# A three-layer decoder block in one Trainium2 core: the value products of two units stand together behind every second score step

## The chip, the cores and the metric

The kernel runs on one core of a Trainium2 chip (trn2). Its time is that of one execution on the device in microseconds (us). The engines are named PE (TensorE; its weight loads are PEld), DVE (VectorE), ACT (ScalarE), POOL (GpSimd) and SP (SyncE, which here only issues DMAs). Each has its own instruction queue, worked off in order, and waits on semaphores that the others raise. The kernel was timed in three runs.

## The reference

Four sequences of 1024 tokens, width 256, 16 heads of 16, all in float32:

```
x = x + self_attention(layernorm(x))      # causal, each chunk of 128 queries sees its own
                                          # 128 keys and those of the chunk before it
x = x + cross_attention(layernorm(x), ctx_1024)   # 77 keys per sequence, masked per query
x = x + ffn(layernorm(x))                 # 8 bit fake-quantised gate, up and down, 704 wide
```

Both attentions are `softmax(q k^T / 4) v` per head, followed by an output projection.

## The kernel before

**Stages.** The attention layers of all four sequences are worked off as sixteen jobs, in the order S0a S0b S1a S1b S2a X0a S2b X0b S3a X1a S3b X1b X2a X2b X3a X3b: S is self attention, X cross attention, the digit is the sequence, and a or b says which eight heads. A job has two phases, g = 0 and g = 1, of four heads each. The feed-forward layer follows when all jobs are done and is not touched here.

**A unit.** In a phase the score matrices are computed transposed (keys on partitions), in units: a self phase has 8 units of 128 keys by 256 queries by 4 heads, a cross phase 4 units of 77 keys by 256 queries by 4 heads. For a unit the step `score` makes four bfloat16 matmuls on PE (L699; cross L706 with a mask matmul L709), ACT takes the exponential out of the two banks into a buffer `pt` (L974, cross L978), and in self attention POOL zeroes what is above the diagonal (L1451). The step `val` then multiplies the exponentials with the values: four float32 matmuls with 17 output columns each (16 of the head and one of ones, which gives the sum), one for each quarter of 32 columns of the PE array (`tile_position=(0, 32 * i)`), at L737 for self and L748 for cross. A float32 matmul is two instructions in the trace, so a unit shows as x8. Unit 3 of a self phase is cut in two halves of 128 queries and shows as x16, unit 7 has only 128 queries. They accumulate in two banks of their own, which ACT copies out after unit 3 (or 1) and after the last one (`evac`, L987).

**What else stands between.** The row maxima of the next phase are found ahead of its scores: score matmuls in the other orientation (`max`, L667 and L670; cross L677 and L679), reduced on DVE (L1179, L1183), turned and sent by ACT's DMA into the rows 96 to 98 of the queries, where the scores subtract them. The projections for the jobs to come (L630, L640), layer normalisation, the output projection (L759), and the weights of the feed-forward layer fill the rest.

**What sets the order.** `attention_order()` writes one list of steps, and every engine works off its part of it in that order. A phase is given a length (24.5 for S, 9.6 for X), and each kind of step a span in it as fractions, in `PLACE`; all steps are sorted by the time that this gives. `score` step j stands at j/8 or j/4 of the phase. `val` of unit j - 2 stands right behind `score` j (`BEHIND["val"]` is 2), and the last two units of a phase, its tail, stand at the span `tail` of the next phase. There are three buffers `pt` (`NPT`), and an exponential waits until the `val` of the score step three before it has been made. In `follow()` further steps are hung behind a step by a number of steps (`norm`, `proj`, `rows`, `acc`, `fin`).

**The keys of cross attention.** The step `xkeys` projects the values of the cross keys (PE L649, DVE adds the bias at L1169, POOL sets the ones at L1446); DVE and POOL wait there for the last `val` of the job before the running one. The step `bulk` copies queries and keys into one of four slots by six DMAs on SP (L523 from `parts`; the cross keys L517 from `kparts`). `PLACE["keys x"]` places `xkeys` and the key copy for g = 0 of the next cross job, where the running job is a cross one; there are four such places (jobs X2a, X2b, X3a and X3b are the next).

Of the kernel before, what the change touches and what calls it, by code (L numbers as in the profile page):

```python
# [6 lines left out]
F32 = mybir.dt.float32  # L7
# [9 lines left out]
KX = 77  # L17
FI = 704
FT = 6
NPT = 3  # L20
NEG = -1.0e30
EPS = 1e-5
SCALE = 0.25
# [3 lines left out]
        for j in "S0a S0b S1a S1b S2a X0a S2b X0b S3a X1a S3b X1b X2a X2b X3a X3b".split()]  # L27
# [5 lines left out]
PLACE = {"max s0s": (-0.001, 0.635), "max s1s": (-0.31, 0.27), "max s1x": (-0.071, 0.513),  # L33
# [6 lines left out]
         "score x": (0.078, 1.077), "shift": (0.305, 1.038), "setup": (0.177, 0.8), "v first": (-0.574, 0.433),  # L40
         "qk first": (0.482, 0.895)}

BEHIND = {"scaled": 3, "turned": 3, "scaled 4": 0, "split": 1, "vmove": 0, "bulk": 13, "turnm": 3, "evac": 4,
          "spread": 2, "gather": 2, "invert": 5, "store": 2, "widen": 8, "scale": 8, "wturn": 2, "val": 2}

# [40 lines left out]
class Order:  # L86
# [5 lines left out]
    def put(self, s):  # L92
        if s[0] == "force":
            while any(g == s[1] for _, g, _ in self.due):
                it = next(it for it in self.due if it[1] == s[1])
                self.due.remove(it)
                self.put_one(it[2])
            return
        self.put_one(s)
        ready = []  # L100
        for it in list(self.due):
            it[0] -= 1
            if it[0] < 0:
                ready.append(it)
        for it in ready:
            if it in self.due:
                self.due.remove(it)
                self.put_one(it[2])
# [12 lines left out]
def over(span, steps):  # L121

    return [(span[0] + (span[1] - span[0]) * i / len(steps), step) for i, step in enumerate(steps)]
# [43 lines left out]
def attention_order():  # L167
# [19 lines left out]
    def put(steps):  # L187
        timed.extend(((start + t * length, len(timed) + i, step) for i, (t, step) in enumerate(steps)))

    for p in range(2 * len(JOBS)):  # L190
# [1 line left out]
        job, units = JOBS[n], UNITS[JOBS[n][0]]  # L192
        kind, length = job[0], LENGTH[job[0]]
        nxt = JOBS[n + 1] if n + 1 < len(JOBS) else None
        put([(-0.001, ("force", "rows"))] + over(PLACE["tail " + kind], tail))
        scores = over(PLACE["score " + kind], [("score", job, g, j) for j in range(units)])
        for j in range(units):
            put([scores[j]])
            if j >= BEHIND["val"]:
                put([(scores[j][0] + 0.002, ("val", job, g, j - BEHIND["val"], False))])  # L200
        tail = [("val", job, g, j, j == units - 1) for j in range(units - BEHIND["val"], units)]
        if p + 1 < 2 * len(JOBS):
            put(over(PLACE[f"max {kind}{g}{nxt[0] if g else kind}"], max_steps(p + 1)))
        last = JOBS[n - 1] if n else ("s", 0, 0)
# [70 lines left out]
def build(nc, x_in, ctx_in, mask_in, w_qkv, w_out, Wq, bq, Wk, bk, Wv, bv, Wo, bo, clip_x, clip_d, w_gate, w_up,  # L275
          w_down, out):
    with ExitStack() as ctx:
        def sb(name, shape, dt):
            return ctx.enter_context(nc.sbuf_tensor(name, shape, dt))
# [8 lines left out]
        ring = big[:, 0:16384].bitcast(BF16).rearrange("p (r z h t) -> p r z h t", r=4, z=2, h=4)  # L288
        qs = [ring[:, r, 0] for r in range(4)]
        ks = [ring[:, r, 1] for r in range(4)]  # L290
        pt = [big[:, 16384 + 1024 * i:17408 + 1024 * i] for i in range(NPT)]
        rem = big[:, 19456:20480].rearrange("p (i n) -> p i n", i=2)
        va = [big[:, 20480 + 1088 * f:21568 + 1088 * f].rearrange("p (c h d) -> p c h d", c=NC, h=8)
              for f in range(2)]
# [1249 lines left out]
```

How the kernel before makes its waits and increments, by code:

```python
        def run_sync(e):  # L480
            e.dma_start(xs[:, 0:4, :], x_dram[:, 0:4, :]).then_inc(ld_x[0], 16)
            e.dma_start(xs[:, 4:8, :], x_dram[:, 4:8, :]).then_inc(ld_x0, 16)
            e.wait_ge(ld_x0, 16)
            e.dma_start(xs[:, NC:2 * NC, :], x_dram[:, NC:2 * NC, :]).then_inc(ld_x[1], 16)
            for i, w in enumerate((Wk, Wv, Wq, Wo)):
                e.dma_start(xwn[:, i], w.rearrange("(c p) n -> p c n", p=128)).then_inc(ld_xw, 16)
# [14 lines left out]
                    e.dma_start(wo[h:128:8, c, :], w_out[c * 128 + 16 * h:c * 128 + 16 * h + 16, :]).then_inc(ld_wo, 16)  # L501
            for s in plan:
                k = s[0]
                if k == "xload":
                    b = s[1]
                    e.dma_start(xs[:, NC * b:NC * b + NC, :], x_dram[:, NC * b:NC * b + NC, :]).then_inc(ld_x[b], 16)
                elif k == "bulk" and s != first_keys:
                    _, job, g, z = s
                    r = slot(job, g)
                    if AT[job] > 1:
                        e.wait_ge(t_val, slot_free(job, g))
                    elif z == 1 and r == 3:
                        e.wait_ge(a_wqkv, 3)
                    if job[0] == "x" and z == 1:
                        e.wait_ge(d_keys, 4)
                        for rr in range(6):
                            e.dma_start(xks[r][rr:96:6, :, :],
                                        kparts[64 * g:64 * g + 64, job[2], K_PART[rr], job[1] * KX:job[1] * KX + KX]
```

## Time and profile before

| | us |
|---|---|
| three timed runs, median | 851.69 |
| lowest and highest | 844.95 and 858.25 |
| profiled execution, first to last instruction | 849.0 |
| PE busy in it | 684.6 (81%) |
| DVE busy | 545.8 (64%) |
| ACT busy | 415.1 (49%) |

The profiled execution has no other time of its own than its span of 849.0 us; it lies 2.7 us under the median. A profile row names the engine, the source line, the operation, output and input, and how often. Where it is a stretch of the timeline, the first number is the start and the second the duration in us, and the bracket at its end names the idle time before and who ended it. The end of a matmul in such a row is modelled and lies behind the moment at which the next one can start, so what a group of matmuls costs its engine is the distance from its start to the start of the next group.

### The profile page before, as it was taken

How to read it: one execution, taken by the hardware profiler on the slowest of the kernel's cores; microseconds unless marked ns; L12 is line 12 of the kernel's file. 1: busy time of each engine (PE TensorE's matmuls, PEld its weight loads, DVE VectorE, ACT ScalarE, POOL GpSimd, SP SyncE). 2: the span in 40 equal slices, each digit the busy share in tenths (PEclk: the TensorE clock that was granted, in tenths of full speed). 3: DMA queues.
4: the chain of work that ended last, by engine and by line, in shares of the span. 5: the costliest groups of instructions: out<-in, count | busy, mean ns of one | idle time of the engine just before them, and what ended most of it. 6: DMA issues, size and time to landing. Idle time of an engine off the chain costs nothing.

```text
span 849.0 us, 14814 instructions
## 1 busy us (share of the span) xinstructions
PE 684.6 (81%) x5391; PEld 414.9 (49%) x5396; DVE 545.8 (64%) x975; ACT 415.1 (49%) x610; POOL 188.8 (22%) x231
## 2 busy tenths in 40 slices
PE   2579999989996998999979989897886784488565
PEld 1346565655653564556644644464543442233254
DVE  6277658866864456677636874556745651679996
ACT  2324665536463444555334446433343352399775
POOL 5002131312231120310113123002002000044436
PEclk9988999999997997999988989997998786699989
DMA  7534243502622153243222432331237112000013
GB/s 215 125 106 143 54 128 81 149 3 90 165 77 61 21 170 105 46 141 78 86 50 96 109 96 69 97 95 42 70 85 211 23 42 53 0 1 2 0 65 135
DMA packets 59557, 71.83 MB, mean 85 GB/s; under 512 B 25003, under 2 KB 36447, under 8 KB 59487
## 3 DMA queue, kind: packets, MB, share of 16 engines
q1 hardware_dynamic: 53391, 68.01, 29.2%
q10 hardware_dynamic: 6096, 2.88, 1.3%
q8 instruction: 44, 0.72, 0.4%
q14 instruction: 26, 0.21, 0.1%
HBM read 17.74 MB, written 4.72 MB: 26 GB/s over the span
## 4 chain that ended last, share of the span: by engine, by line
PE 49%; DVE 22%; issue 8%; ACT 7%; SPq 6%; DMA 6%; ACTq 1%; POOL 1%; POOLq 0%; DVEq 0%
PE banks L630 8%; PE banks L759 7%; PE banks L667 5%; PE banks L737 5%; DVE mneg L1179 4%; PE banks L699 4%; PE banks L640 3%; PE banks L748 3%; SPq L523 3%; PE banks L670 3%; DVE xn L1143 2%; SPq L517 2%; PE banks L706 2%; PE banks L709 2%; DVE tops L1358 2%
## 5 line engine op out<-in xcount | busy, mean ns | idle before, releaser
L1179 DVE TENSOR_REDUCE mneg<-banks 128x4 f32<-128x1024 f32 (+1 forms) x128 | 145.1, 1151 | 68.0 <-PE banks L670 67.5
L974 ACT ACTIVATE big<-banks 128x1024 f32<-128x1024 f32 (+1 forms) x128 | 123.0, 974 | 105.4 <-PE banks L699 101.7
L1451 POOL TENSOR_SCALAR_AFFINE_SELECT big<-big 128x512 f32<-128x512 f32 x128 | 83.1, 650 | 391.6 <-ACT big L974 390.9
L978 ACT ACTIVATE big<-banks 77x1024 f32<-77x1024 f32 x64 | 65.3, 1020 | 86.3 <-PE banks L709 81.8
L667 PE MATMUL banks<-big 96*128 96x256 bf16 (+1 forms) x512 | 94.5, 280 | 13.4 <-DMA big<-parts 9.8
L630 PE MATMUL banks<-xnT,weights 128*128 128x512 f32 x192 | 92.9, 617 | 3.9 <-ACT big L978 3.9
L699 PE MATMUL banks<-big 99*128 99x256 bf16 (+1 forms) x512 | 79.3, 280 | 13.3 <-DMA big<-m3t 5.7
L1183 DVE TENSOR_REDUCE mneg<-banks 128x8 f32<-128x616 f32 x64 | 50.3, 793 | 57.7 <-PE banks L679 57.6
L737 PE MATMUL banks<-big 128*17 128x256 f32 (+1 forms) x1152 | 79.0, 366 | 1.0 <-POOL big L1451 0.6
L670 PE MATMUL banks<-causal,identb 128*128 128x256 bf16 x256 | 72.9, 288 | 0.0
L667 PEld LDWEIGHTS banks<-big 96*128 96x128 bf16 x512 | 47.9, 103 | 45.9 <-issue 26.6
L699 PEld LDWEIGHTS banks<-big 99*128 99x128 bf16 x512 | 45.0, 101 | 48.3 <-issue 32.5
L803 PE MATMUL banks<-oe,weights 128*128 128x512 bf16 x187 | 46.8, 394 | 11.0 <-DVE big L1352 4.4
L630 PEld LDWEIGHTS banks<-xnT,weights 128*128 128x128 f32 x192 | 35.7, 197 | 38.1 <-issue 31.4
L677 PE MATMUL banks<-big 96*128 96x77 bf16 x512 | 43.1, 214 | 13.2 <-DMA big<-kparts 9.6
L706 PE MATMUL banks<-big 99*77 99x256 bf16 x256 | 51.1, 282 | 3.1 <-DVE big L1169 1.1
L677 PEld LDWEIGHTS banks<-big 96*128 96x128 bf16 x512 | 35.3, 108 | 32.9 <-issue 19.8
L709 PE MATMUL banks<-maskt,identb 77*77 77x512 bf16 x128 | 50.4, 394 | 0.0
L987 ACT COPY oe<-banks 128x512 f32<-128x512 f32 x64 | 37.2, 585 | 26.8 <-DMA oTx<-oe 10.9
L1224 DVE TENSOR_TENSOR xs<-banks,xs 128x512 f32<-128x512 f32 x32 | 22.1, 689 | 37.6 <-PE banks L759 37.6
L618 PE MATMUL banks<-ident,xn 128*128 128x128 f32 x128 | 23.7, 319 | 23.9 <-DVE xn L1143 23.5
L748 PE MATMUL banks<-big 77*17 77x256 f32 x512 | 42.7, 426 | 0.0
(155 smaller groups left out, 1163.8 us busy)
## 6 DMA issues: line engine op xcount, KB each, us to landing
big<-parts SPq DMA_DIRECT2D x282, 128.0 KB, 2.5
oc<-sums SPq DMA_DIRECT2D x16, 512.0 KB, 4.6
oTs<-oe SPq DMA_DIRECT2D x64, 64.0 KB, 2.3
out_dram<-oTs SPq DMA_DIRECT2D x16, 256.0 KB, 2.1
xs<-in_x_dram SPq DMA_DIRECT2D x3, 1024.0 KB, 5.8
big<-oe SPq DMA_DIRECT2D x32, 64.0 KB, 2.3
oTx<-oe SPq DMA_DIRECT2D x32, 64.0 KB, 2.3
big<-kparts SPq DMA_DIRECT2D x96, 9.6 KB, 1.8
```

The costliest lines, as they stand in the source:

```text
L630: t = e.matmul(bank(p), w[:, i, :], xnT[T][:, i, blk * 512:blk * 512 + 512], start=(i == 0), stop=(i == 1))
L667: e.matmul(bank(p, j)[:, i * 256 + lo * 128:i * 256 + 256], Q[0:96, hh, c * 128:c * 128 + 128], K[0:96, hh, (c - 1 + lo) * 128:(c + 1) * 1 ...
L670: t = e.matmul(bank(p, j).rearrange("p (s n) -> p s n", s=2)[:, :, 128:256], identb[:, :], causal[:, :].rearrange("p (a n) -> p a n", a=1) ...
L677: e.matmul(bank(p, j)[:, i * KX:i * KX + KX], Q[0:96, i, (c + j) * 128:(c + j) * 128 + 128], xks[r][0:96, i, :], start=(i == 0), stop=Fals ...
L699: t = e.matmul(bank(p, i // 2)[:, (i % 2) * 256:(i % 2) * 256 + n], ks[r][0:99, i, j * 128:j * 128 + 128], qs[r][0:99, i, j * 128:j * 128 ...
L706: e.matmul(bank(p, z)[0:KX, i * 256:i * 256 + 256], xks[r][0:99, 2 * z + i, :], qs[r][0:99, 2 * z + i, j * 256:j * 256 + 256], start=(i == ...
L709: t = e.matmul(bank(p, z)[0:KX, :].rearrange("p (i n) -> p i n", i=2), identb[0:KX, 0:KX], keep.to_broadcast([KX, 2, 256]), start=False, s ...
L737: t = e.matmul(acc[:, col // 512][32 * i:32 * i + 17, col % 512:col % 512 + z - a], va[f][:, j, 4 * g + i, :], P[:, i, a:z], start=new, st ...
L748: t = e.matmul(acc[:, j // 2][32 * i:32 * i + 17, (j % 2) * 256:(j % 2) * 256 + 256], xv[r][0:KX, i, 0:17], pt[u][0:KX, i * 256:i * 256 + ...
L974: e.activation(pt[u].rearrange("p (i n) -> p i n", i=4)[:, :, 0:n], pair(p).rearrange("p j (s n) -> p (j s) n", s=2)[:, :, 0:n], ACT.Exp, ...
L1179: e.tensor_reduce(M.rearrange("p (h c) -> p h c", h=4)[:, :, c], pair(p).rearrange("p j (s n) -> p (j s) n", s=2)[:, :, lo * 128:256], AX. ...
L1451: e.affine_select(out=P[:, :, 0:128], in_=P[:, :, 0:128], compare_op=ALU.is_ge, fill=0.0, base=0, pattern=[[0, 4], [1, 128]], channel_mult ...
```

## The change

The `val` steps are no longer put one behind each score step. Behind each odd score step j from 3 on stand those of the units j - 3 and j - 2; the tail of a phase is its last two units, as before, and both stand at the start of the tail's span. An exponential now stays in its buffer for up to four score steps, so there are six buffers, the three new ones in a tensor `more` of 12 KB per partition. The memory for it comes from the scratch that is set aside for DMAs, which is cut to 1024 bytes per partition. The place of `xkeys` and of its key copy moves from before the start of the phase to just behind the tail.

```diff
-NPT = 3
+NPT = 6
...
-         "bulk x": (0.192, 0.576), "keys s": (0.673, 0.862), "keys x": (-0.198, -0.165), "out ss": (0.981, 1.432),
+         "bulk x": (0.192, 0.576), "keys s": (0.673, 0.862), "keys x": (0.02, 0.06), "out ss": (0.981, 1.432),
...
-          "spread": 2, "gather": 2, "invert": 5, "store": 2, "widen": 8, "scale": 8, "wturn": 2, "val": 2}
+          "spread": 2, "gather": 2, "invert": 5, "store": 2, "widen": 8, "scale": 8, "wturn": 2, "val": 3}
...
-        put([(-0.001, ("force", "rows"))] + over(PLACE["tail " + kind], tail))
+        put([(-0.001, ("force", "rows"))] + [(PLACE["tail " + kind][0], step) for step in tail])
         scores = over(PLACE["score " + kind], [("score", job, g, j) for j in range(units)])
         for j in range(units):
             put([scores[j]])
-            if j >= BEHIND["val"]:
-                put([(scores[j][0] + 0.002, ("val", job, g, j - BEHIND["val"], False))])
-        tail = [("val", job, g, j, j == units - 1) for j in range(units - BEHIND["val"], units)]
+            if j % 2 and j >= BEHIND["val"]:
+                put([(scores[j][0] + 0.002, ("val", job, g, j - BEHIND["val"] + i, False)) for i in range(2)])
+        tail = [("val", job, g, j, j == units - 1) for j in range(units + 1 - BEHIND["val"], units)]
...
-        pt = [big[:, 16384 + 1024 * i:17408 + 1024 * i] for i in range(NPT)]
+        more = sb("more", [128, 3, 1024], F32)
+        pt = [big[:, 16384 + 1024 * i:17408 + 1024 * i] for i in range(3)] + [more[:, i, :] for i in range(3)]
...
-    nc = _bacc.Bacc("TRN2", target_bir_lowering=False, num_devices=1)
+    nc = _bacc.Bacc("TRN2", target_bir_lowering=False, num_devices=1, dynamic_dma_scratch_size=1024)
```

How this moves instructions is seen at three places. Source lines of the changed kernel are one higher from the new tensor on.

PE in a self phase, from a step of the value projection (L640) on, before and with the change. L699 is `score`, L737 is `val`, L667 and L670 are `max`, L589 turns weights.

```order
L640 MATMUL banks<-weights,xnT 128x128 x8
L699 MATMUL banks<-big 128x256 x4
L737 MATMUL banks<-big 17x256 x4
L667 MATMUL banks<-big 128x256 x2
L670 MATMUL banks<-causal,identb 128x2x128
```

```order
L641 MATMUL banks<-weights,xnT 128x128 x8
L700 MATMUL banks<-big 128x256 x4
L668 MATMUL banks<-big 128x256 x2
L671 MATMUL banks<-causal,identb 128x2x128
```

Behind this score step no `val` stands any more, and `max` follows `score` directly.

PE at the end of the same phase: units 2 and 3 of self attention.

```order
L699 MATMUL banks<-big 128x256 x4
L737 MATMUL banks<-big 17x256 x4
L699 MATMUL banks<-big 128x256 x4
L737 MATMUL banks<-big 17x128 x8
L589 MATMUL banks<-ident,oc 128x128 x2
L687 MATMUL banks<-identb,m 96x128
```

```order
L700 MATMUL banks<-big 128x256 x8
L738 MATMUL banks<-big 17x256 x4
L738 MATMUL banks<-big 17x128 x8
L688 MATMUL banks<-identb,m 96x128
L590 MATMUL banks<-ident,oc 128x128 x2
```

Two score steps now follow one another, and then two `val` steps. In the whole program the `val` steps stand in 168 unbroken groups on PE before (116 begin with L737, 52 with L748) and in 106 with the change (69 and 37).

SP, the DMA queue, in the cross jobs (`spread` of the output of X1b is oTx<-oe, query copies are L523, key copies L517, the store of the sums L542).

```order
L535 DMA oTx<-oe 16x1024 x4
L517 DMA big<-kparts 16x4x77 x6
L523 DMA big<-parts 16x4x1024 x12
L517 DMA big<-kparts 16x4x77 x6
L535 DMA oTx<-oe 16x1024 x4
L542 DMA sums<-ls 128x64
```

```order
L536 DMA oTx<-oe 16x1024 x4
L524 DMA big<-parts 16x4x1024 x6
L518 DMA big<-kparts 16x4x77 x6
L524 DMA big<-parts 16x4x1024 x6
L536 DMA oTx<-oe 16x1024 x4
L518 DMA big<-kparts 16x4x77 x6
L543 DMA sums<-ls 128x64
```

The key copy for g = 0 now stands behind the query copy for g = 0 and no longer ahead of it; the number of DMAs is the same. On DVE, L1169 moves behind one reduction of the maxima (L1183) and what stands ahead of it at the same places.

## Rows read from the trace of the kernel before

**Rows 1.** The page: span, busy time of the engines, DMA queues.

```profile
span 849.0 us, 14814 instructions
PE 684.6 (81%) x5391; PEld 414.9 (49%) x5396; DVE 545.8 (64%) x975; ACT 415.1 (49%) x610; POOL 188.8 (22%) x231
q1 hardware_dynamic: 53391, 68.01, 29.2%
q10 hardware_dynamic: 6096, 2.88, 1.3%
```

**Rows 2.** Stretches: length, PE, PEld, DVE, ACT, POOL busy, granted clock, DMA share, GB/s.

```profile
94.00:165.00 71.00, 68.93 (x625) 42.08 (x625) 48.53 (x79) 43.55 (x74) 18.29 (x28) 1.00 0.40 114
60.00:650.00 590.00, 525.82 (x4502) 322.04 (x4502) 376.33 (x686) 280.55 (x410) 120.16 (x169) 0.93 0.34 93
```

**Rows 3.** The page's chain that ended last, by line, and costliest groups.

```profile
PE banks L630 8%; PE banks L759 7%; PE banks L667 5%; PE banks L737 5%; DVE mneg L1179 4%; PE banks L699 4%; PE banks L640 3%; PE banks L748 3%; SPq L523 3%; PE banks L670 3%; DVE xn L1143 2%; SPq L517 2%; PE banks L706 2%; PE banks L709 2%; DVE tops L1358 2%
...
L737 PE MATMUL banks<-big 128*17 128x256 f32 (+1 forms) x1152 | 79.0, 366 | 1.0 <-POOL big L1451 0.6
...
L748 PE MATMUL banks<-big 77*17 77x256 f32 x512 | 42.7, 426 | 0.0
```

**Rows 4.** Timeline of PE in self attention, start and duration.

```profile
111.50 0.61 PE L699 MATMUL banks<-big 99*128 99x256 bf16 x4
111.95 0.38 PE L667 MATMUL banks<-big 96*128 96x256 bf16 x2
...
161.47 0.60 PE L699 MATMUL banks<-big 99*128 99x256 bf16 x4
162.00 0.63 PE L737 MATMUL banks<-big 128*17 128x256 f32 x8
162.56 0.39 PE L667 MATMUL banks<-big 96*128 96x256 bf16 x2
```

**Rows 5.** Timeline of PE in both attentions, where two units already stand together.

```profile
315.73 1.06 PE L748 MATMUL banks<-big 77*17 77x256 f32 x16
316.72 0.41 PE L706 MATMUL banks<-big 99*77 99x256 bf16 x2
```

**Rows 6.** Waits, longest first: us in total, times, longest.

```profile
POOL big L1451 <- ACT big L974: 390.9, 119, 44.7
ACT big L974 <- PE banks L699: 101.7, 63, 7.8
...
PE banks L677 <- DMA big<-kparts: 9.6, 2, 4.9
```

**Rows 7.** What L737's engine sat idle for, in all.

```profile
  issue: 21.2, 94
  POOL big L1451: 5.0, 14
```

**Rows 8.** Timeline of DVE and PE at two of the four steps xkeys.

```profile
530.40 0.35 DVE L1169 TENSOR_TENSOR big<-banks,bvb 77x64 f32<-77x64 f32 x2 [5.03 <-PE banks L737]
...
564.37 0.35 DVE L1169 TENSOR_TENSOR big<-banks,bvb 77x64 f32<-77x64 f32 x2 [4.24 <-PE banks L748]
564.77 0.41 PE L706 MATMUL banks<-big 99*77 99x256 bf16 x2 [0.57 <-DVE big L1169]
```

**Rows 9.** Timeline of SP, the DMA queue, in the cross jobs.

```profile
551.20 2.40 SPq L535 DMA_DIRECT2D oTx<-oe  x4
553.70 3.94 SPq L517 DMA_DIRECT2D big<-kparts  x6
557.74 10.29 SPq L523 DMA_DIRECT2D big<-parts  x12
```

**Rows 10.** Timeline of PE behind a low clock.

```profile
578.82 1.06 PE L748 MATMUL banks<-big 77*17 77x256 f32 x8
579.81 0.44 PE L677 MATMUL banks<-big 96*128 96x77 bf16 x4
```

**Rows 11.** Stretches behind two waits of PE, columns as in rows 2.

```profile
268.00:278.00 10.00, 7.99 (x48) 5.02 (x46) 3.83 (x4) 1.02 (x1) 0.64 (x1) 0.52 0.15 44
278.00:289.00 11.00, 11.00 (x63) 6.60 (x62) 4.75 (x7) 5.09 (x8) 1.27 (x2) 1.00 0.01 1
```

## The prediction

> **What bounds the kernel now.** I read the page first, then the stretches, then the chain of waits, and the timeline last. The page says that PE is busy for 81% of the span, and DVE, next, for 64% [rows 1]. That is a mean over stages with different limits. The stretches show the stage that the change touches: from 94 to 165 us PE is busy for 68.93 of 71 us, from 60 to 650 us for 525.82 of 590, or 89%, while DVE has 64% there and ACT 48% [rows 2]. So in the attention jobs PE sets the pace, with some 64 us of holes. The chain agrees in part: L737 and L748, the `val` steps, are some 8% of the span on it, 68 us, out of 79.0 + 42.7 = 121.7 us of busy time [rows 3]. About 56% of the `val` time lies on the chain; the rest is in places where PE has to wait later anyway.
>
> **What a `val` group costs.** Arithmetic is not changed: the same number of matmuls, exponentials and selects is made. What falls is the number of times that PE goes from full-width matmuls to the quarter-width `val` matmuls and back, from 168 groups to 106, 62 fewer. The price of a group is read from start to start. Four score matmuls with a `val` next take 162.00 - 161.47 = 0.53 us, with L667 next 111.95 - 111.50 = 0.45 us, so entering costs 0.08 us. One `val` unit takes 162.56 - 162.00 = 0.56 us until the next group starts [rows 4]. Two units that already stand together take 316.72 - 315.73 = 0.99 us [rows 5], so the second costs 0.43 us, and 0.56 - 0.43 = 0.13 us is what leaving costs once per group. In sum 0.21 us per group, and 62 x 0.21 = **13.0 us** if PE never waited.
>
> I weigh it by the share of PE's time that counts. The lower end is the chain's share, 0.56 x 13.0 = 7.3 us; the upper is the busy share of the stretch, 0.89 x 13.0 = 11.6 us. The two differ because the chain takes only one way through, and a shorter PE would still shift other ways. I take the middle, **9.4 us**. Nothing else hides these gaps: the weight loads that follow a `val` group start only when it is over, which is the "issue" idle of PE's loads ahead of L737, 21.2 us in 94 cases [rows 7].
>
> Of the same gap the Trainium skill, "TensorE: Matmul & The Clock Gate", section "Single matmul latency", says that the time for a result to drain out of the array is about 175 ns whatever the columns, and "TensorEngine Tiling (Array Packing)", section "Key Properties", that changing the tiling mode drains the engine. By one such drain per removed group, an estimate from these pages, 10.9 us would be the full price instead of 13.0; the rows are higher and are used above.
>
> **Waits of `val`.** The loads of L737 sat idle for POOL's select 5.0 us in 14 cases, of which PE itself 0.6 us [rows 3, 7]. The first unit of each pair now has one more score step of lag, the second the same as before. Bounds are 0 and 5.0; I take 0.6, what PE itself stood still for. ACT's waits for a free buffer cannot grow: with six buffers it waits for the `val` six score steps back, made before. ACT waits 101.7 us for L699 and POOL 390.9 us for ACT [rows 6], so both have room for two score steps that now come together.
>
> **xkeys.** DVE stood 5.03 and 4.24 us at two of the four places for the last `val` of the job before, and what was queued behind it were the maxima and the output additions; PE stood 0.57 us behind it at one [rows 8]. Now the step stands behind the tail and DVE gets other work first. What that gives is bounded by 0 and by the 9.3 us of these two waits. DVE has 36% of the stretch free, so I take 1.1 us, twice the wait that PE shows.
>
> **Moves on SP.** At four places the key copy for g = 0 goes behind the query copy for g = 0. Six of the one take 3.94 us to issue, twelve of the other 10.29, so 5.1 us for six [rows 9]. In the row, 553.70 + 5.1 + 3.94 = 562.7 us would be the end of the key copy, and the first `max` that reads it is at 579.81 us [rows 10]: 17 us of cover. Without that cover it would cost PE up to 5.1 us each time. The store of the sums goes behind another six key copies once, 3.9 us, covered by the phase that lies between it and its use. I cost both at nothing.
>
> **Memory and tail.** The packets of the data are on queues of the kind hardware_dynamic [rows 1], and POOL issues no DMA, so the cut scratch is cost at 0. The Trainium skill, "SBUF — State Buffer", section "SBUF size: 192, 224, or 256?", describes this scratch as the ring for descriptors written by software; no run here has such a DMA. The tail of a phase stands together and at most half a microsecond earlier; zero.
>
> **Sum.** 9.4 + 0.6 + 1.1 = 11.1 us, from a span of 849.0 to 837.9 us. The median of the runs shown is 2.7 us above that span, so the time is 840.6, and I say **840.5 us**, 1.3% less. What a measurement of this kernel can tell from no change is about 2%, 17 us: 834.7 and 868.7 us are the limits.
>
> **Rivals.**
> - *Absorbed.* PE arrives earlier at waits of fixed length (landings, DVE's chains of small operations) and stands there. For it: PE already waited 9.6 us in two cases for a landing of keys [rows 6], and only 56% of `val` is on the chain. It would leave 3 us or so of the 13.0, 848.5 us. Against it: 89% busy, and long stretches without a hole. Chance 0.22.
> - *More than the sum.* All of the removed time counts, and DVE's and the selects' waits go as well: 13.0 + 5.0 + 9.3 = 27.3 us at most, 824 us; with two thirds of that, 833 us. For it: DVE's two long stands held the maxima back, on which two later phases rest, and with fewer holes PE may keep its clock. Chance 0.22.
> - *Slower: SP becomes late.* SP is issuing without a break from 551 to 568 us [rows 9]. If the query copy that now stands first has to wait for its input, the key copy waits behind it and PE stands at the first `max` of a phase. It decides once the query copy waits by more than the 17 us of cover; then each of the four places costs between one set of six, 5.1 us, and both, 9.0 us: 851.7 - 11.1 + 4 x 5.1 = 861 us, or 876.6 us by the upper price. Against it is the cover. Chance 0.04.
> - *Slower: the clock.* Behind two waits PE's granted clock was 0.52 in a stretch of 10 us and 1.00 again in the next [rows 11]; one `val` unit behind another such fall took 579.81 - 578.82 = 0.99 us instead of 0.56 [rows 4, 10]. A PE that has less to do and the same waits could fall to the low level, 1.2 GHz, more often: each 10 us stretch at half costs some 5 us, and from three such stretches on the gain is gone; four give 851.7 - 11.1 + 20 = 860.6 us. The Trainium skill, the page on TensorE named above, section "HAM oscillation — how this bites in real kernels", puts such falls down to stands of PE between bursts of matmuls. By that rule a kernel that waits more would lose its gain. Against it: the work taken out is standing time of PE inside its bursts, not work, so its stands at waits grow by 3.6 us in all at most (13.0 - 9.4). Chance 0.05.
>
> **How the numbers follow.** Forecast, 0.47: 835 to 845 us, by the two ends of each term and the spread of the three runs. Absorbed 0.22, more 0.22, slower 0.09. The range from **826 to 852 us** leaves out the slower rivals and the far end of "more". Faster by over 2% is nearly all of "more" and a small end of the forecast, 0.24; slower by over 2% is a third of the slower cases, 0.03; within 2% is 0.73.
>
> **What would show it.** In the changed kernel the timeline of PE should have x16 or two adjoining rows at L738 and L749 with 0.99 us to the next group, 106 groups, and 0.44 us for four scores ahead of a `max`. The "issue" idle before L738 and L749 should fall by a third. DVE's waits at L1170 should be under 2 us in all. PE's busy time should fall a little and its holes of over 0.3 us stay. Wrong would be: long waits of PE for kparts or parts, more stretches at half clock, or a longer idle of PE before the `val` steps for ACT or POOL. If the exchanges are gone and the span is not shorter by at least 7 us, the share that I gave to PE was too high.

## The result, and the profile after

The changed kernel took **871.37 us** (median of 4 runs, 870.41 to 874.51), the kernel before 854.65 us (4 runs on the same chip, 844.95 to 858.25). The ratio is **1.0232**, with an interval from 1.0159 to 1.0305. The chip has a faster and a slower state whatever the kernel, and all ratios compare only runs in the faster one, so that they differ a little from what the medians give. Forecast were 840.5 us in a range of 826 to 852. The prediction was wrong in sign and size. In the experiments below the kernel before had medians of 846.84 to 850.28 us; ratios are always against runs on the same chip.

The page of the changed kernel (lines of the change have moved by one: `val` is L738 and L749, `score` L700 and L707):

```profile
span 872.3 us, 14826 instructions
PE 690.0 (79%) x5391; PEld 432.7 (50%) x5396; DVE 544.8 (62%) x975; ACT 414.5 (48%) x610; POOL 189.2 (22%) x231
...
L700 PE MATMUL banks<-big 99*128 99x256 bf16 (+1 forms) x512 | 75.0, 276 | 17.8 <-DMA big<-m3t 7.9
```

Against [rows 1] the span is 23.3 us longer and PE is busy for 5.4 us more, although it goes less often from full-width to quarter-width matmuls and back (an exchange, below). The price of a group of `val` was read rightly. The timeline of PE, where a pair stands:

```profile
120.45 0.60 PE L700 MATMUL banks<-big 99*128 99x256 bf16 x4
120.99 1.06 PE L738 MATMUL banks<-more,big 128*17 128x256 f32 x16
121.98 0.28 PE L668 MATMUL banks<-big 96*128 96x256 bf16 x1
```

It is 0.54 and 0.99 us from start to start, as in [rows 4, 5]. The groups by line, PE's weight loads of `val`, then its matmuls in self attention (busy | idle before):

```profile
L738 PEld LDWEIGHTS banks<-more,big 128*17 128x17 f32 x584 | 14.2, 98 | 13.7 <-issue 5.2 <-POOL more L1452 1.7
L738 PEld LDWEIGHTS banks<-big 128*17 128x17 f32 x568 | 11.8, 96 | 15.6 <-issue 6.3 <-POOL big L1452 4.7 <-POOL more L1452 0.4
...
L738 PE MATMUL banks<-big 128*17 128x256 f32 (+1 forms) x568 | 36.1, 357 | 1.2 <-POOL big L1452 0.7
L738 PE MATMUL banks<-more,big 128*17 128x256 f32 (+1 forms) x584 | 34.0, 344 | 0.5 <-POOL more L1452 0.5
```

The "issue" idle of the loads fell from 21.2 [rows 7] to 11.5 us, and `val` in self attention keeps PE busy for 70.1 instead of 79.0 us [rows 3]. So the saving happened. Where the time went shows in two stretches: from 60 us to the first exponential of the all-cross jobs (X2a), and from there to the last exponential of attention. Columns as in [rows 2]; the kernel before:

```profile
60.00:545.60 485.60, 439.43 (x3821) 269.91 (x3821) 314.61 (x556) 240.53 (x353) 105.49 (x153) 0.94 0.34 93
545.60:702.50 156.90, 123.21 (x929) 74.92 (x929) 91.28 (x198) 62.91 (x104) 16.32 (x17) 0.86 0.32 81
```

The changed kernel:

```profile
60.00:551.80 491.80, 429.39 (x3820) 277.52 (x3820) 313.16 (x556) 238.97 (x354) 105.83 (x153) 0.95 0.33 91
551.80:723.80 172.00, 135.81 (x920) 84.06 (x920) 91.57 (x198) 63.50 (x103) 16.30 (x17) 0.75 0.29 74
```

In the **first stretch** PE works 10.0 us less and stands idle for 62.4 instead of 46.2 us, 16.2 us more: in all 6.2 us longer. In the **all-cross stretch** PE stands 36.2 instead of 33.7 us, but is busy for 12.6 us more with no more work, at a mean granted clock of 0.75 instead of 0.86: 15.1 us longer. The two make 21.3 of the 23.3 us.

One place has 4.3 of these 15.1 us (the end of the stretch loses about as much). From the exponential ahead of a stand of PE to one some 30 us on, before and in the changed kernel:

```profile
607.80:636.40 28.60, 22.98 (x211) 12.94 (x208) 16.56 (x35) 11.86 (x17) 2.81 (x4) 0.94 0.41 102
617.30:650.20 32.90, 28.09 (x211) 16.33 (x212) 17.19 (x37) 12.79 (x18) 3.02 (x6) 0.74 0.34 84
```

The timeline of PE there, then the 16 us behind its stands, in the changed kernel:

```profile
621.50 0.32 PE L678 MATMUL banks<-big 96*128 96x77 bf16 x4 [4.22 <-DVE mneg L1184]
...
622.94 0.44 PE L678 MATMUL banks<-big 96*128 96x77 bf16 x4 [0.61 <-DVE big L1170]
```

```profile
622.00:638.00 16.00, 15.39 (x110) 8.62 (x108) 6.52 (x18) 3.90 (x5) 0.00 (x0) 0.50 0.32 78
```

and in the kernel before, at the same step:

```profile
611.73 0.32 PE L677 MATMUL banks<-big 96*128 96x77 bf16 x4 [3.37 <-DVE mneg L1183]
```

```profile
612.00:628.00 16.00, 14.37 (x127) 8.41 (x124) 8.51 (x21) 5.23 (x8) 0.00 (x0) 0.89 0.38 101
```

PE is busy for most of the 16 us in both, but at a granted clock of 0.50 it makes 110 matmul instructions instead of 127. The second stand, of 0.61 us, is for the bias of the moved `xkeys` (L1170). Before, a wait for the same line (0.57 us at 606.71 us) stood ahead of the long stand, not behind it. The clock fell behind the long stand in the kernel before as well, but came back soon:

```profile
612.00:616.00 4.00, 4.00 (x29) 2.79 (x26) 3.29 (x8) 1.02 (x1) 0.00 (x0) 0.57 0.62 197
```

**One of the new waits.** `turnm` (the turning of the maxima on PE, L687, with ACT's copy L962 and its DMA L964 behind it) is hung three steps behind `rows`. Before, one of these three steps was a `val` at the place shown here; in the changed order it is a score step. By the two lists of steps, 5 of the 32 `turnm` steps have one score step more ahead of them. The timeline of ACT at this one of the five, before:

```profile
486.81 1.02 ACT L978 ACTIVATE big<-banks 77x1024 f32<-77x1024 f32 x1 [0.19 <-PE banks L709]
487.73 0.61 ACT L943 CAST parts<-big 128x512 bf16<-128x512 f32 x1
488.24 0.26 ACT L962 COPY m3t<-banks 96x128 bf16<-96x128 bf16 x1
488.53 0.78 ACTq L964 DMA_DIRECT2D big<-m3t  x1
489.42 1.02 ACT L978 ACTIVATE big<-banks 77x1024 f32<-77x1024 f32 x1 [0.92 <-PE banks L748]
...
491.55 0.60 PE L699 MATMUL banks<-big 99*128 99x256 bf16 x4 [2.04 <-DMA big<-m3t]
```

and in the changed kernel, with PE's row of the first score that reads the result (as the last row above):

```profile
489.77 1.02 ACT L979 ACTIVATE big<-banks 77x1024 f32<-77x1024 f32 x1 [0.19 <-PE banks L710]
490.69 0.61 ACT L944 CAST parts<-big 128x512 bf16<-128x512 f32 x1
491.20 1.02 ACT L979 ACTIVATE more<-banks 77x1024 f32<-77x1024 f32 x1
492.12 0.26 ACT L963 COPY m3t<-banks 96x128 bf16<-96x128 bf16 x1
492.40 0.79 ACTq L965 DMA_DIRECT2D big<-m3t  x1
...
496.33 1.01 PE L700 MATMUL banks<-big 99*128 99x256 bf16 x4 [4.12 <-DMA big<-m3t]
```

Before, the DMA went out ahead of the next exponential, now behind it, and PE stands 4.12 instead of 2.04 us. Nothing in `val` itself is at fault there: a step beside it was counted into another place.

### The profile page after: what moved, and what is told of

Read it like the earlier page. It is cut to its first block, busy times and chain, and to the rows that moved or that the text cites. A ratio compares the mean times of both kernels' runs of the same rounds, so it can differ in the third digit from the quotient of the medians.

```text
span 872.3 us, 14826 instructions
## 1 busy us (share of the span) xinstructions
PE 690.0 (79%) x5391; PEld 432.7 (50%) x5396; DVE 544.8 (62%) x975; ACT 414.5 (48%) x610; POOL 189.2 (22%) x231
## 4 chain that ended last, share of the span: by engine, by line
PE 26%; DVE 13%; issue 5%; DMA 4%; SPq 4%; ACT 3%; POOL 1%; ACTq 0%; POOLq 0%; DVEq 0%
PE banks L760 6%; PE banks L749 3%; PE banks L631 2%; PE banks L707 2%; SPq L518 2%; PE banks L710 2%; DMA oc<-sums 2%; PE banks L678 2%; PE banks L680 1%; DVE tops L1359 1%; DVE mneg L1180 1%; PE banks L804 1%; PE banks L668 1%; DMA big<-m3t 1%; DVE big L1353 1%
## 5 line engine op out<-in xcount | busy, mean ns | idle before, releaser
L1180 DVE TENSOR_REDUCE mneg<-banks 128x4 f32<-128x1024 f32 (+1 forms) x128 | 144.9, 1151 | 77.5 <-PE banks L671 77.2
L668 PE MATMUL banks<-big 96*128 96x256 bf16 (+1 forms) x512 | 95.1, 282 | 18.7 <-DMA big<-parts 10.2
L975 ACT ACTIVATE big<-banks 128x1024 f32<-128x1024 f32 (+1 forms) x65 | 62.9, 979 | 67.2 <-PE banks L700 67.1
L700 PE MATMUL banks<-big 99*128 99x256 bf16 (+1 forms) x512 | 75.0, 276 | 17.8 <-DMA big<-m3t 7.9
L1452 POOL TENSOR_SCALAR_AFFINE_SELECT big<-big 128x512 f32<-128x512 f32 x65 | 43.3, 666 | 201.0 <-ACT big L975 200.8
L1452 POOL TENSOR_SCALAR_AFFINE_SELECT more<-more 128x512 f32<-128x512 f32 x63 | 40.2, 638 | 195.7 <-ACT more L975 195.2
L975 ACT ACTIVATE more<-banks 128x1024 f32<-128x1024 f32 (+1 forms) x63 | 59.1, 961 | 47.5 <-PE banks L700 46.6
L668 PEld LDWEIGHTS banks<-big 96*128 96x128 bf16 x512 | 48.9, 104 | 47.3 <-issue 29.0
L700 PEld LDWEIGHTS banks<-big 99*128 99x128 bf16 x512 | 45.9, 100 | 42.3 <-issue 28.4
L707 PE MATMUL banks<-big 99*77 99x256 bf16 x256 | 55.0, 300 | 3.9 <-DMA big<-m3t 2.6
L979 ACT ACTIVATE big<-banks 77x1024 f32<-77x1024 f32 x31 | 31.6, 1019 | 54.0 <-PE banks L710 51.5
L678 PEld LDWEIGHTS banks<-big 96*128 96x128 bf16 x512 | 36.8, 112 | 35.4 <-issue 19.6
L710 PE MATMUL banks<-maskt,identb 77*77 77x512 bf16 x128 | 54.0, 422 | 0.0
L979 ACT ACTIVATE more<-banks 77x1024 f32<-77x1024 f32 x33 | 33.4, 1019 | 39.5 <-PE banks L710 39.5
```

The lines of the kernel that those rows point to most:

```text
L668: e.matmul(bank(p, j)[:, i * 256 + lo * 128:i * 256 + 256], Q[0:96, hh, c * 128:c * 128 + 128], K[0:96, hh, (c - 1 + lo) * 128:(c + 1) * 1 ...
L678: e.matmul(bank(p, j)[:, i * KX:i * KX + KX], Q[0:96, i, (c + j) * 128:(c + j) * 128 + 128], xks[r][0:96, i, :], start=(i == 0), stop=Fals ...
L700: t = e.matmul(bank(p, i // 2)[:, (i % 2) * 256:(i % 2) * 256 + n], ks[r][0:99, i, j * 128:j * 128 + 128], qs[r][0:99, i, j * 128:j * 128 ...
L707: e.matmul(bank(p, z)[0:KX, i * 256:i * 256 + 256], xks[r][0:99, 2 * z + i, :], qs[r][0:99, 2 * z + i, j * 256:j * 256 + 256], start=(i == ...
L710: t = e.matmul(bank(p, z)[0:KX, :].rearrange("p (i n) -> p i n", i=2), identb[0:KX, 0:KX], keep.to_broadcast([KX, 2, 256]), start=False, s ...
L975: e.activation(pt[u].rearrange("p (i n) -> p i n", i=4)[:, :, 0:n], pair(p).rearrange("p j (s n) -> p (j s) n", s=2)[:, :, 0:n], ACT.Exp, ...
```

## The experiments

Each edit is to the kernel before unless something else is said. "Groups" are groups of `val` on PE.

**Memory alone** (six buffers, smaller scratch, the old order).

```diff
-NPT = 3
+NPT = 6
...
+        more = sb("more", [128, 3, 1024], F32)
+        pt = [big[:, 16384 + 1024 * i:17408 + 1024 * i] for i in range(3)] + [more[:, i, :] for i in range(3)]
...
+    nc = _bacc.Bacc("TRN2", target_bir_lowering=False, num_devices=1, dynamic_dma_scratch_size=1024)
```

> The kernel before with six buffers and the smaller scratch, order of steps unchanged. Theory A (order of the val steps costs the time): 0.995 to 1.005 of before. Theory B (where the buffers lie or the cut scratch cost it): 1.01 to 1.03.

Measured: 854.74 us, 1.0059 [0.9998, 1.0120], between the two theories. It is not the bulk of the loss, but a cost of some tenths of a per cent is not ruled out.

**Pairs in self or in cross phases alone**, by the change's rule, with this memory; `xkeys` and its key copy at the old place in the first, at the new one in the second.

```diff
+PAIRED = {"s": True, "x": False}
...
-            if j >= BEHIND["val"]:
-                put([(scores[j][0] + 0.002, ("val", job, g, j - BEHIND["val"], False))])
+            if PAIRED[kind]:
+                if j % 2 and j >= 3:
+                    put([(scores[j][0] + 0.002, ("val", job, g, j - 3 + i, False)) for i in range(2)])
+            elif j >= 2:
+                put([(scores[j][0] + 0.002, ("val", job, g, j - 2, False))])
```

> Pairs in self phases only, six buffers; cross phases and xkeys as before. Theory A1 (the loss is made in the cross jobs, where the granted clock falls; the self jobs give back what they save in waits for DVE and ACT): 0.995 to 1.01. Theory A2 (pairs are bad wherever they stand, by their longer unbroken work without a score): 1.01 to 1.02. Theory C (xkeys moved is the cause): under 1.0, some 0.99, since the 47 removed groups of 0.21 us are then a gain.

> Pairs in cross phases and xkeys at its new place; self phases as before. Theory A1: 1.015 to 1.025, nearly the whole loss, with more of the low clock from 545 us on. Theory A2: about 1.005 to 1.01, a share by the number of groups, 15 of 62. Theory C: as A1, so it needs the next kernel to tell it apart.

Measured: self 849.37 us, 1.0057 [1.0015, 1.0098]; cross 873.21 us, 1.0339 [1.0227, 1.0451]. The cross kernel had 4 runs: three of 872.57 to 873.81 us give the ratio, and the fourth, of 1998.46 us, is left out; the only profile is of that one and is not used. The loss is on the cross side, which here has the moved key steps too, and in self phases, where most of the gain was forecast, there is none.

**The key steps alone** (nothing paired, three buffers).

```diff
-"keys x": (-0.198, -0.165)
+"keys x": (0.02, 0.06)
```

> The kernel before with xkeys and its key copy at the new place and nothing else. Theory C (the step moved costs: the key copy behind the query copy on SP, the values' bias later on DVE): 1.01 to 1.02. Theory A1 or A2 (the pairs cost): 0.995 to 1.005, DVE's waits at L1169 fall from 10.5 us to under 4.

Measured: 859.21 us, 1.0189 [1.0074, 1.0305], 4 runs: most of the change's loss by point, with a wide interval. (A few steps hung behind others shift with them; `val` stands in 172 groups.) The timelines of SP, of ACT and of PE show one place where the queue becomes late:

```profile
636.01 4.10 SPq L523 DMA_DIRECT2D big<-parts  x6
640.21 2.43 SPq L535 DMA_DIRECT2D oTx<-oe  x4
...
644.47 0.58 ACT L987 COPY oe<-banks 128x512 f32<-128x512 f32 x1 [8.34 <-DMA oTx<-oe]
...
646.07 0.41 PE L677 MATMUL banks<-big 96*128 96x77 bf16 x4 [7.05 <-issue]
```

The spread of `oe` stands behind the query copy on SP, ACT waits 8.34 us for it with its exponentials queued behind, and PE stands 7.05 us. In this kernel it is the rival "SP becomes late", by another transfer than the one that it named: the one queued behind is the spread of `oe`, and the one that waits first is ACT.

**Pairs with the key copy early**, and **each key step moved alone**.

```diff
-                    put(over(PLACE["keys " + kind], [("xkeys", nxt), ("bulk", nxt, 0, 1)]))
+                    if kind == "x":
+                        put([(0.02, ("xkeys", nxt)), (-0.1815, ("bulk", nxt, 0, 1))])
+                    else:
+                        put(over(PLACE["keys " + kind], [("xkeys", nxt), ("bulk", nxt, 0, 1)]))
```

That is `xkeys` late; the other kernel has -0.198 and 0.04 instead.

> The whole change, but the key copy for g = 0 stays at its old place ahead of the query copy; xkeys is at the new one. Theory S (the key copy behind the query copy makes SP late by some 4 us at each of four places, spread and then ACT's copy out of oe wait for it): 0.995 to 1.008, the loss of 2.3% gone. Theory K (the pairs themselves cost in the cross jobs, over the granted clock): 1.015 to 1.025. Theory X (xkeys late is what costs): 1.015 to 1.025.

> The kernel before with only the key copy moved behind the query copy, xkeys and all val steps as before. Theory S: 1.01 to 1.02. Theories K and X: 0.995 to 1.005.

> The kernel before with only xkeys moved behind the tail, the key copy as before. Theory S: 0.99 to 1.005, DVE's 10.5 us of waits at this step fall. Theory X: 1.01 to 1.02. Theory K: 0.995 to 1.005.

Measured: pairs with the copy early 866.57 us, 1.0197 [1.0151, 1.0243]; only the copy late 853.19 us, 1.0035 [1.0001, 1.0069]; only `xkeys` late 853.90 us, 1.0066 [1.0021, 1.0110]. My theory of the moment, SP, explains 0.35%, and with the key copy early 1.0197 of the change's 1.0232 stay: it fell as the main cause.

**Single `val` steps three scores late in self phases** (memory as in the change).

```diff
+        lag = 3 if kind == "s" else 2
...
-            if j >= BEHIND["val"]:
-                put([(scores[j][0] + 0.002, ("val", job, g, j - BEHIND["val"], False))])
+            if j >= lag:
+                put([(scores[j][0] + 0.002, ("val", job, g, j - lag, False))])
```

> Self phases with each val three score steps late and alone, three vals in the tail, six buffers; cross phases as before. Theory L (what the pairs save in self phases is lost because val is late, not because it is doubled): 1.005 to 1.015. Theory B (the bunching makes PE wait for banks that ACT and DVE free, the lag does not): 0.995 to 1.005.

Measured: 850.31 us, 1.0020 [0.9977, 1.0063]. Lateness of `val` in self phases costs nothing that shows.

**The clock, by matmuls added at waits.** 28 full-width matmuls are put ahead of each output projection of X2 and X3, and 24 ahead of each of two waits for scale factors of the feed-forward layer; their results are overwritten. The first kernel has pairs in cross phases alone with the copy early, without added matmuls; then come the kernel before, the changed kernel, and the pairs in self phases, each with them.

```diff
+                    if kind == "x" and b >= 2 and c == 0:
+                        hold(p, 28)
...
+                    e.wait_ge(d_out, n_of["out", "x", NB - 1, NC - 2])
+                    hold(p, 24)
```

> Pairs in cross phases only, xkeys late as the pairs need it, the key copy early; self phases as before. If the pairs of the cross phases themselves cost: 1.012 to 1.02, above the 1.0066 of xkeys late alone. If the sum of the change is only self pairs and the moved steps: 1.005 to 1.008.

> The kernel before, with 28 matmuls of 512 columns more on PE ahead of its wait at the output projections of X2 and X3, and 24 more ahead of the two waits for the scale factors of the feed-forward layer; their results are overwritten. Theory G (waits cost twice, once as such and once by the low clock behind them): 0.98 to 0.99. Rival (the low clock is not in the path): 0.998 to 1.005, or more if the added matmuls outlast the waits.

> The whole change with the same added matmuls. Theory G, with the clock the larger part of the loss: 1.0 to 1.01 of before, some 10 us less than the change has over the same kernel with added matmuls only. Rival (the waits themselves are the loss): 1.02 to 1.025.

> Pairs in self phases only, with the same added matmuls. The same as the kernel before with them, within 0.005, as pairs in self phases alone were 1.0057; a version to beat both if Theory G holds, 0.98 to 0.995.

Measured: cross pairs 863.59 us, 1.0207 [1.0156, 1.0258], just above both ranges; before with matmuls 846.10 us, 0.9989 [0.9943, 1.0034]; changed with matmuls 868.76 us, 1.0268 [1.0209, 1.0326]; self with matmuls 846.52 us, 1.0009 [0.9969, 1.0050]. The granted clock rose, in the profiled executions from 0.911 to 0.937 (before) and from 0.892 to 0.911 (changed), and no time came of it. I took this for the end of the clock as a cause, too early: the matmuls stood at other waits. At the place shown above, the clock was still at its low level, by the stretches of the changed kernel with them:

```profile
622.00:638.00 16.00, 15.39 (x112) 8.65 (x112) 6.76 (x17) 3.91 (x5) 0.00 (x0) 0.52 0.30 76
```

**Only the grouping.** The step list of before, with the memory of the change, is left as it is, and only the first `val` of each pair is moved next to the second, in both kinds (96 groups), in cross alone (148) and in self alone (116).

```diff
+    for s in [s for s in o.steps if s[0] == "val" and s[3] % 2 and s[1][0] in 'sx']:
+        first = ("val", s[1], s[2], s[3] - 1, False)
+        o.steps.remove(first)
+        o.steps.insert(o.steps.index(s), first)
```

> The order of the kernel before, step for step, except that the first val of each pair is taken out and put directly ahead of the second: 96 groups instead of 168, xkeys and all steps that are hung behind others by a number of steps stay. Theory H (the pairs cost because the count of steps to a hung step now spans another score, so the maxima are turned and sent later): 0.985 to 0.998, the 72 x 0.21 = 15 us at least in part. Theory P (two val together hurt in themselves, by banks and ACT): 1.005 to 1.02.

> The same regrouping in cross phases only, 148 groups. Theory H: 0.994 to 1.0. Theory P: 1.01 to 1.02, as with pairs by the new rule in cross phases, 1.0207.

> The same regrouping in self phases only, 116 groups. Theory H: 0.988 to 0.998. Theory P: 1.0 to 1.01.

Measured: both 852.32 us, **1.0000** [0.9959, 1.0040]; cross 853.18 us, 1.0051 [1.0011, 1.0092] (one run of 939.15 us left out); self 847.93 us, 0.9990 [0.9949, 1.0030]. 72 exchanges fewer, 72 x 0.21 = 15.1 us on PE, bring nothing against the kernel before. That is between the ranges of theory H (0.985 to 0.998) and theory P (1.005 to 1.02). Against the kernel with the memory alone, at 1.0059 [0.9998, 1.0120], it would be a gain of some 5 us by point, with intervals that overlap. The stretches of the first of these kernels, cut at the same steps:

```profile
60.00:543.00 483.00, 427.52 (x3819) 278.18 (x3816) 312.83 (x555) 238.82 (x354) 104.83 (x153) 0.95 0.34 93
543.00:702.30 159.30, 121.18 (x920) 78.21 (x920) 90.94 (x198) 62.81 (x103) 16.32 (x17) 0.82 0.31 80
```

PE has 11.9 us less to do in the first stretch and stands 9.3 us more; 2.6 us are left, and the all-cross stretch takes 2.4 us back. That is the absorbed rival, which was to leave 3 us or so: the interval allows 3.

**`turnm` one step earlier in the changed kernel**, to mend the wait that the timelines of ACT show.

```diff
-"turnm": 3
+"turnm": 2
```

> The whole change, with the turning of the maxima hung 2 steps behind their rows instead of 3. Theory H with this step as the main one: 1.005 to 1.015, a third to two thirds of the loss gone. If another hung step or the moved xkeys carries the loss: 1.02 to 1.027.

Measured: 880.51 us, 1.0365 [1.0311, 1.0419], 1.3% worse than the change. The waits from 60 to 560 us, here and in the changed kernel (total, times, longest):

```profile
PE banks L688 <- DVE m L1200: 24.8, 13, 3.1
```

```profile
PE banks L688 <- DVE m L1200: 8.8, 11, 1.4
```

The wait of the scores for `m3t` did fall in this stretch, from 7.9 to 3.5 us, but at 13 places PE now stood for maxima that were not ready, for 16.0 us more, so the step stood too early there. A count of steps that fits one place does not fit another.

**The key steps late on the grouped kernel**, nothing else shifted, and **the changed kernel with its `val` steps single again** (159 groups; all other steps in the changed kernel's order).

```diff
+    for n in range(2, len(JOBS)):
+        if JOBS[n][0] == "x" and JOBS[n - 1][0] == "x":
+            end = ("val", JOBS[n - 2], 1, UNITS[JOBS[n - 2][0]] - 1, True)
+            for step in (("bulk", JOBS[n], 0, 1), ("xkeys", JOBS[n])):
+                o.steps.remove(step)
+                o.steps.insert(o.steps.index(end) + 1, step)
```

```diff
+    for s in [s for s in o.steps if s[0] == "val" and s[3] % 2 == 0 and s[3] + 2 < UNITS[s[1][0]]]:
+        o.steps.remove(s)
+        o.steps.insert(o.steps.index(("score", s[1], s[2], s[3] + 2)) + 1, s)
```

> The kernel before in its own order of steps, with the first val of each pair moved next to the second (96 groups instead of 168), and then only the xkeys step and the g=0 key copy of each cross job moved right behind the end val of the job before the running one, in jobs that follow a cross job. No other step is shifted. Theory keys (what is lost hangs on where the keys of the next job are made and spread): 1.010 to 1.025 of the kernel before, most of the change's 1.0232, with the DVE and SP copies later in the cross section. Theory shift (what is lost is lost by the other hung steps, which count steps and so move when val steps move): 1.000 to 1.010, the key steps alone having cost 1.0066 and 1.0035 when each was moved by itself.

> The changed kernel with every other step exactly where the changed kernel has it, but with the first val of each pair taken out of its pair and put behind the score step before it, so that val steps are single again (159 groups instead of 106). Theory shift (the order of the other steps holds the loss, the grouping itself neither gains nor loses): 1.018 to 1.030 of the kernel before, the same as the change's 1.0232. Theory pairs (two units together, or their longer lateness, are what costs): 1.000 to 1.010. Something between says that both take part.

Measured: keys late on the grouped kernel 858.84 us, **1.0135** [1.0083, 1.0187]; changed kernel with single steps 876.43 us, **1.0371** [1.0323, 1.0418]. The second, above both of its ranges, says that the order of the other steps costs, the moved key steps among them, and more than the whole loss. With the pairs the same order is at 1.0232, so in it the grouping gains 1.4%, about 11.8 us of 849, where 159 - 106 = 53 groups at 0.21 us are 11.1 us. (The single steps also stand at other places among the scores than the pairs do, so that not all of the 1.4% need be exchanges.) Its first stretch:

```profile
60.00:560.90 500.90, 443.02 (x3821) 272.58 (x3820) 314.84 (x556) 240.89 (x354) 105.39 (x153) 0.94 0.33 90
```

PE is busy about as long as before (443.0 and 439.4 us) and stands 57.9 instead of 46.2 us.

The first lies, by point, in the range of theory "keys" (1.010 to 1.025) and above that of theory "shift" (1.000 to 1.010). Nothing but the steps that the diff names is moved in it, so they cost 1.35%, about 11.4 us, on the grouped order: by point, more than half of the loss. The steps that shift with them are left with the way from 1.0135 to 1.0232, about 8 us; the two intervals overlap. Single steps show this part beyond the intervals, 1.0371 [1.0323, 1.0418] against 1.0189 [1.0074, 1.0305] with the key steps alone (the second kernel is without the memory of the change, which has 0.6% by point). The profiled spans point the same way: 850.0 us grouped, 860.4 with the keys late, 872.3 with the change.

What the moved key steps do is seen against the grouped kernel as the neighbour. Its stretches, and then the timeline of SP and PE (cross `max` is L688 there and L682 in the neighbour):

```profile
60.00:545.30 485.30, 431.07 (x3821) 279.43 (x3820) 313.25 (x556) 239.17 (x354) 105.75 (x153) 0.95 0.34 93
545.30:712.70 167.40, 129.79 (x920) 82.52 (x920) 91.53 (x198) 63.16 (x104) 16.30 (x17) 0.78 0.29 76
...
612.00:632.00 20.00, 19.09 (x128) 11.38 (x126) 9.09 (x23) 4.60 (x6) 0.00 (x0) 0.50 0.32 82
```

```profile
604.23 4.04 SPq L534 DMA_DIRECT2D big<-parts  x6
608.36 3.74 SPq L528 DMA_DIRECT2D big<-kparts  x6
...
611.74 0.42 PE L688 MATMUL banks<-big 96*128 96x77 bf16 x4 [4.22 <-DVE mneg L1194]
...
613.84 0.44 PE L688 MATMUL banks<-big 96*128 96x77 bf16 x4 [0.91 <-DVE big L1180]
```

and those of the grouped kernel with the keys at the old place, from the same step on, then cut where its clock came back:

```profile
611.00:631.00 20.00, 19.48 (x172) 12.18 (x170) 10.54 (x24) 9.30 (x15) 0.00 (x0) 0.90 0.43 111
...
609.00:615.00 6.00, 4.25 (x29) 3.19 (x30) 5.07 (x11) 1.02 (x1) 0.00 (x0) 0.50 0.61 205
615.00:631.00 16.00, 15.48 (x145) 9.24 (x144) 7.47 (x17) 8.28 (x14) 0.00 (x0) 1.00 0.38 87
```

```profile
603.59 4.03 SPq L522 DMA_DIRECT2D big<-kparts  x6
607.72 7.64 SPq L528 DMA_DIRECT2D big<-parts  x12
...
610.75 0.44 PE L682 MATMUL banks<-big 96*128 96x77 bf16 x4 [3.37 <-DVE mneg L1188]
```

The all-cross stretch is 8.1 us longer, with PE's stands 37.6 and 38.1 us, the same, and its busy time 8.6 us longer. PE is equally busy in the 20 us shown (19.1 and 19.5), but makes 128 matmul instructions instead of 172, at a granted clock of 0.50, the level of 1.2 GHz, instead of 0.90. The clock fell at the stand in both. In the grouped kernel it was back from 615 us on; with the keys late it stayed low to 632 us. Ahead of that, PE stood for 4.22 us instead of 3.37 and then once more, for 0.91 us, for the bias of the moved `xkeys` (L1180). Which of the two held the clock down, or what PE had to do next, no run tells apart. The length of the first stand is not all: behind the same 3.37 us the clock of the kernel before was low for a shorter time (0.57 over 4 us, shown above) than that of the grouped one (0.50 over 6). So in this pair of profiles the moved steps cost little as waits, and the clock that follows carries the time.

## Why the prediction was wrong

**What failed.** Two terms. The first is the moved steps, for which the sum had a gain of 1.1 us from `xkeys` and, on SP, "I cost both at nothing". On the grouped order these two moves cost 1.35%, about 11.4 us, and 8.1 of the 10.4 us between the profiled spans are in the all-cross stretch, at a lower clock. In this step only the steps that the diff names were counted. The change also shifts steps that it does not name: `turnm` and others are hung behind a step by a number of steps, and the number counts `val` steps. They have the rest, about 8 us. I priced no such step, and put no rival to it. The second term is the share of 9.4 us that I gave to PE: 1.0000 in the old order.

**The price of a group** was right (0.54 and 0.99 us against 0.53 and 0.99), so were the 106 groups, and "issue" fell by 30% in all, nearly all of it in self: 21.2 us in self [rows 7] and 14.1 in cross have become 11.4 and 13.2.

**PE's share** was wrong in the old order. The absorbed rival left 3 us of 13.0, the runs with the grouping alone 0 of 15.1, with 9.3 us more of stands in the first stretch. The signs were the waits for keys [rows 6] and that only 56% of `val` lay on the chain [rows 3]; a busy share of 89% says how much PE has to do, not that it is next when that falls. In the changed order the same saving seems to have counted in full (1.0371 to 1.0232). The weight of a saving belongs to an order, not to an engine.

**Waits of `val`**, 0.6 us of gain: PE's own wait for POOL went from 0.6 to 1.2 us, that of the loads, by the view of [rows 7], from 5.0 to 7.9. No gain, and no loss that matters.

**xkeys**, 1.1 us of gain: DVE's two waits of [rows 8] are gone. What is left is, by DVE's line of it:

```profile
L1170 DVE TENSOR_TENSOR big<-banks,bvb 77x64 f32<-77x64 f32 x16 | 2.8, 214 | 4.7 <-PE banks L650 4.7
```

These 4.7 us are waits for its own matmul, so the 2 us that I wrote for all waits of this line was too low. Its move alone costs 0.66%, some 5.6 us, instead of bringing 1.1.

**Moves on SP**, at nothing: the key copy late costs 0.35% alone, 3 us. The cover of 17 us held: PE's waits for `kparts` are 7.2 us in the changed kernel and were 9.6 [rows 6]. I had looked at the first reader of the key copy only, not at what else stands behind the query copy in the queue, such as the spread of `oe`, for which ACT waits with its exponentials.

**The clock**, chance 0.05: its price was about right and its condition wrong. By the mean clock of the all-cross stretch, the time at the low level is 156.9 x 0.14 / 0.5 = 44 us before and 172 x 0.25 / 0.5 = 86 us after, 42 us more: about the four stretches that I priced at 20 us together, and PE is busy for 12.6 us more. I held it unlikely since "its stands at waits grow by 3.6 us in all at most". They grew by 18.7 us: by 16.2 in the first stretch, where the mean clock did not fall (0.95 and 0.94), and by 2.5 only in the all-cross stretch, where it did. The rule on standing between bursts that the prediction cited from the Trainium skill, "TensorE: Matmul & The Clock Gate", section "HAM oscillation — how this bites in real kernels", agrees with the trace here as far as the fall goes: 0.50 behind stands of 3.37 and of 4.22 us. What I set against it, the sum of the stands, is not what the rows go by. Over the runs the same shows: in the 80 timings of the kernel before that the ratios use, the time falls by 5.5 us for each 0.01 of granted clock (mean 847.5 us at 0.913). The four runs of the changed kernel have 0.891, which makes about 12 us by that line, and lie some 12 us above it. Which part the clock causes and which it only follows isn't settled by this.

**What stays open.** Which of the hung steps cost how much: the wait for `m3t` is one that the traces show, and moving it by one step made others worse. And what keeps the clock low behind a stand, and whether the all-cross stretch would be short with the clock held up there: no matmuls were put at these stands. The parts don't add up either: `xkeys` and the copy each alone make 1.0%, both 1.9% [0.7, 3.1] in one kernel. No version beat the kernel before; the nearest are at 0.9989 and 0.9990, the same within their intervals.

## What to carry to other kernels

Before pricing a change of an order, list each step whose place is counted from the steps that are moved, and compare the two orders at the places where an engine already waits: what is queued behind the named steps is not the only thing that moves. To learn what an idea is worth, make the edit without the planner, one pair of steps at a time with the rest of the list fixed; here that took apart the grouping (no gain), the named moves (1.35%) and the rest. Where PE stands for some microseconds ahead of a full stretch, count what a fall to 1.2 GHz takes from that stretch, and look for a second wait right behind the stand: here such a place, with the same sum of stands over the whole stretch, went with 8 us more.

## What was not expected of the hardware

- Adding matmuls at four waits of PE raised the mean granted clock in the profiled executions from 0.911 to 0.937, and the time was at 0.9989 [0.9943, 1.0034] of before. A mean clock says little without the place.
- 72 exchanges between full-width and quarter-width matmuls, 15.1 us of PE's time, taken out of the attention jobs, with PE busy for 90% of the first stretch: 1.0000 [0.9959, 1.0040].
- With PE busy for 19.1 of 20 us, the clock stayed at 0.50 for all of them, behind stands of 4.22 and 0.91 us. At the same place, behind one stand of 3.37 us, it fell too, but was back at 1.00 after some 4 us of work.
